# Mamba mixer on one core: the input norm moved to the end of the chunk two ahead of its own

## What is computed

```
def _ln_c(v, eps=1e-6):                      # over the 384 channels
    m = jnp.mean(v, axis=1, keepdims=True)
    s = jnp.var(v, axis=1, keepdims=True)
    return (v - m) / jnp.sqrt(s + eps)

xz = xseq @ in_proj_w.T                      # xseq = _ln_c(x); 384 -> 2 x 768
xin, z = jnp.split(xz, 2, axis=-1)
u = silu(causal_conv3(xin) + conv_b)         # per channel, 3 taps
dbc = u @ x_proj_w.T                         # dt (24), B (16), C (16)
dt = softplus(dt @ dt_proj_w.T + dt_proj_b)
# per position, 768 channels x 16 states:
h = exp(dt * A) * h + (dt * u) * B
y = sum_n h * C
out = x + ((y + u * D) * silu(z)) @ out_proj_w.T
```

## Time and profile before

| what | value |
|---|---|
| median of 3 runs | 3678.46 us (3677.39 to 3678.49) |
| profiled execution: span, first to last instruction | 3674.1 us |
| busy in the span: PE, DVE, ACT, POOL | 3352.4, 3256.0, 2759.3, 2577.3 us |
| the same, share | 91%, 89%, 75%, 70% |
| mean granted TensorE clock | 0.969 of 2.4 GHz |

### The profile page before, as it was taken

One profiled execution on the slowest core, in us unless ns is written; L12 is line 12 of the kernel. 1 busy time (PEld: TensorE's weight loads), 2 busy tenths in 40 slices (PEclk: granted clock), 3 DMA queues, 4 the chain that ended last, 5 costly groups with the idle time before them and its releaser, 6 DMA issues. The chain is left out here.

```text
span 3674.1 us, 50128 instructions
## 1 busy us (share of the span) xinstructions
PE 3352.4 (91%) x16962; PEld 2370.5 (65%) x16962; DVE 3256.0 (89%) x3376; ACT 2759.3 (75%) x5350; POOL 2577.3 (70%) x2045
## 2 busy tenths in 40 slices
PE   6989989899999989899989989898889998889997
PEld 3666666666666666666666666666657776557776
DVE  3999999999999999999999999999967887876886
ACT  5888797888789788977978787888655554875553
POOL 3898988989898988989898988989921111551100
PEclk7999999999999999999999999999999999999998
DMA  3020211202020211202020210202111113641212
GB/s 134 10 92 19 92 38 65 85 18 85 19 92 19 92 47 55 84 18 85 19 98 23 83 69 33 84 19 85 63 58 35 53 53 143 236 184 40 70 36 87
DMA packets 83586, 249.89 MB, mean 68 GB/s; under 512 B 15212, under 2 KB 24044, under 8 KB 73092
## 3 DMA queue, kind: packets, MB, share of 16 engines
q1 hardware_dynamic: 82564, 245.65, 18.6%
q10 hardware_dynamic: 768, 1.05, 0.1%
HBM read 204.73 MB, written 41.95 MB: 67 GB/s over the span
## 5 line engine op out<-in xcount | busy, mean ns | idle before, releaser
L956 POOL TENSOR_TENSOR slot<-dtu,b_rep 128x512 f32<-128x512 f32 x960 | 1206.4, 1277 | 78.5 <-PE ysum L454 77.8
L966 POOL TENSOR_TENSOR slot<-slot,c_rep 128x512 f32<-128x512 f32 x768 | 974.1, 1278 | 157.3 <-ACT carry L763 92.5
L454 PE MATMUL ysum<-ident,slot 128*128 128x128 f32 x6144 | 831.4, 280 | 31.9 <-POOL slot L966 16.7
L454 PEld LDWEIGHTS ysum<-ident,slot 128*128 128x128 f32 x6144 | 725.9, 145 | 173.0 <-issue 103.1
L754 ACT ACTIVATE state<-dt,aneg 128x512 f32<-128x512 f32 x960 | 655.4, 688 | 237.9 <-DVE slot L1065 200.8
L1065 DVE TENSOR_TENSOR slot<-state,c_rep 128x512 f32<-128x512 f32 x768 | 514.3, 672 | 0.0
L572 PEld LDWEIGHTS state<-diag_b,dtu_t 128*128 128x128 f32 x3072 | 385.0, 194 | 130.3 <-issue 121.1
L572 PE MATMUL state<-diag_b,dtu_t 128*128 128x128 f32 x3072 | 422.7, 281 | 33.0 <-ACT carry L763 16.6
L745 ACT ACTIVATE slot<-dt,aneg 128x512 f32<-128x512 f32 x576 | 405.4, 711 | 23.1 <-PE ysum L454 23.0
L1057 DVE TENSOR_TENSOR_SCAN slot<-state,slot 128x512 f32<-128x512 f32 x288 | 343.3, 1209 | 44.1 <-ACT state L754 33.6
L1057 DVE TENSOR_TENSOR_SCAN slot<-state,carry,slot 128x512 f32<-128x512 f32 x288 | 360.6, 1269 | 6.3 <-POOL slot L956 3.3
(11 more groups left out here) (272 smaller groups left out, 6291.9 us busy)
## 6 DMA issues: line engine op xcount, KB each, us to landing
c_rep<-rows_of_b_and_c SPq DMA_DIRECT2D x64, 1024.0 KB, 5.1
xres_l<-between_layers SPq DMA_DIRECT2D x18, 1536.0 KB, 9.8
xn_l<-between_layers SPq DMA_DIRECT2D x13, 1536.0 KB, 7.1
b_rep<-rows_of_b_and_c SPq DMA_DIRECT2D x16, 1024.0 KB, 4.5
between_layers<-y SPq DMA_DIRECT2D x10, 1536.0 KB, 6.4
xn<-in_x SPq DMA_DIRECT2D x16, 768.0 KB, 4.5
b_rep<-rows_of_b_and_c SPq DMA_DIRECT2D x16, 768.0 KB, 4.1
xres<-in_x SPq DMA_DIRECT2D x16, 768.0 KB, 4.5
```

Source lines behind the costliest of these rows:

```text
L454: last = mm(ysum[:, cols], slot[:, (NS * k + n) % SLOTS, cols], ident[:], start=first and j == 0, stop=final, is_transpose=True, skip_grou ...
L956: tt(slot[:, q % SLOTS], dtu[:, k % 2], b_rep[:, b_row(n)], ALU.mult).then_inc(dbu_done, 1)
L966: tt(slot[:, q % SLOTS], slot[:, q % SLOTS], c_rep[:, n], ALU.mult).then_inc(pool_mult_done, 1)
```

## The change

The norm of chunk d = c + 2 now stands at the end of chunk c, at steps 81 (mean), 86 (center), 90 (square), 89 (variance), 95 (rstd) and 93 (scale), for c = 0 to 13. Only the norm of chunk 1 stays where it was, in chunk 0 (`FIRST_NORM_AT`). The squares go into `acc`, the convolution's three tiles, which are free once the silus of chunk c + 1 are through; so the residual's load no longer waits for the variance, only for the store before it. The turn of B moves from step 80 to 83, the first turn of dt u from 84 to 87. Waits for py are exchanged: the mean waits for the fifth gate's silu, the output projection into py for the norm, the first in-projection for a residual copy. All instructions are the same in number and size.

```diff
--- before.py
+++ after.py
@@ -36,7 +36,8 @@
 OUT_IN, RES_AT = (BX, BY, BX), (13, 14, 22)
 LAST_OUT_IN, EARLY_OUT_AT, LATE_OUT_AT = (BX, BY, BZ), (88, 82, 84), (89, 90, 91)
 X_SUM_AT = 86
-MEAN_AT, CENTER_AT, SQUARE_AT, VAR_AT, RSTD_AT, SCALE_AT = 18, 21, 25, 25, 31, 28
+MEAN_AT, CENTER_AT, SQUARE_AT, VAR_AT, RSTD_AT, SCALE_AT = 81, 86, 90, 89, 95, 93
+FIRST_NORM_AT = (18, 21, 25, 25, 31, 28)
 GATE_AT, GATE_IN = (20, 22, 37, 49, 62, 70), (BX, BZ, BY, BX, BY, BZ)
 IN_AT, IN_IN = (28, 33, 34, 39, 45, 47), (BY, BZ, BX, BX, BY, BZ)
 CONV_IN_AT, CONV_AT = (33, 38, 41, 46, 50, 54), (31, 37, 40, 45, 50, 51)
@@ -48,8 +49,8 @@
 DT_ADD_AT = (67, 72, 77, 92, 30, 38)
 EARLY = 4
 DT_U_AT = 4
-TURN_U_AT, COPY_U_AT = (84, 13, 29, 44, 60, 75), (95, 20, 36, 48, 68, 84)
-TURN_B_AT, COPY_B_AT = 80, 90
+TURN_U_AT, COPY_U_AT = (87, 13, 29, 44, 60, 75), (95, 20, 36, 48, 68, 84)
+TURN_B_AT, COPY_B_AT = 83, 90
 DIAG_AT = (91, 94, 4, 9, 2, 7)
 HALO_AT = 20
 
@@ -168,7 +169,7 @@
         halo_mid = sb("halo_mid", [P, KT, 1])
         halo_bias = sb("halo_bias", [P, KT, 2])
 
-        sq = xres
+        sq = acc
         xp = sb("xp", [P, T])
         rl = sb("rl", [P, EARLY, T])
         dt = sb("dt", [P, KT, T])
@@ -244,9 +245,7 @@
 
             def load_res(b, h):
                 c = 2 * b + h
-                if not isinstance(c, int) or c < NCHUNK - 1:
-                    sp.wait_ge(var_full, c + 2)
-                else:
+                if later(c):
                     sp.wait_ge(x_stored, 16 * c)
                 nc.sync.sem_inc(res_free, 1)
                 sp.dma_start(xres[:], XV[b, :, :, h * T:(h + 1) * T]).then_inc(xres_loaded, 16)
@@ -327,7 +326,7 @@
             def norm_mean(d, h, image):
                 pe.wait_ge(x_loaded[h], 16 * (image + 1))
                 if later(d, 1):
-                    pe.wait_ge(res_done, CT * (d - 2) + 2)
+                    pe.wait_ge(z_read, KT * (d - 2) + 5)
                 if isinstance(d, int) and d == 1:
                     pe.wait_ge(dt_read, 2)
                 for t in range(CT):
@@ -343,6 +342,8 @@
             def in_proj(d, h, m):
                 if m == 0:
                     pe.wait_ge(normed, d + 1)
+                    if later(d, 1):
+                        pe.wait_ge(res_done, CT * (d - 2) + 2)
                 if m == 1 and later(d):
                     pe.wait_ge(u_copied, KT * (d - 1) + 3)
                 if m == 2 and later(d):
@@ -429,7 +430,10 @@
                         pe.wait_ge(out_w_in, 16)
                         pe.wait_ge(gated, KT * c + KT - 1)
                     if k == 0 and m == 1:
-                        pe.wait_ge(z_read, KT * (c + 1))
+                        if c < NCHUNK - 2:
+                            pe.wait_ge(normed, c + 3)
+                        else:
+                            pe.wait_ge(z_read, KT * (c + 1))
                     if k == 0 and m == 2 and banks == OUT_IN:
                         pe.wait_ge(res_done, CT * c + 1)
                     if k == 0 and m == 2 and banks != OUT_IN:
@@ -609,10 +613,14 @@
                             gate_proj(c, h, k)
                         if after and q == IN_AT[k]:
                             in_proj(d, 1 - h, k)
-                    if after and q == MEAN_AT:
-                        norm_mean(d, 1 - h, b + h)
-                    if after and q == VAR_AT:
-                        norm_var(d)
+                    if c == 0 and q == FIRST_NORM_AT[0]:
+                        norm_mean(1, 1, 0)
+                    if c < NCHUNK - 2 and q == MEAN_AT:
+                        norm_mean(c + 2, h, b + 1)
+                    if c == 0 and q == FIRST_NORM_AT[3]:
+                        norm_var(1)
+                    if c < NCHUNK - 2 and q == VAR_AT:
+                        norm_var(c + 2)
                     if after and q == XP_AT:
                         x_proj(d, 1 - h)
                     if not after:
@@ -665,8 +673,8 @@
 
             def norm_square(d, h):
                 act.wait_ge(centered, d + 1)
-                if later(d, 1):
-                    act.wait_ge(x_stored, 16 * (d - 1))
+                if later(d):
+                    act.wait_ge(u_done, KT * d)
                 af(sq[:], xn[:, h], ACT.Square).then_inc(squared, 1)
 
             def norm_rstd(d):
@@ -859,10 +867,14 @@
                                     set_diag(c, h, i)
                             elif after:
                                 set_diag(d, 1 - h, i)
-                    if after and q == SQUARE_AT:
-                        norm_square(d, 1 - h)
-                    if after and q == RSTD_AT:
-                        norm_rstd(d)
+                    if c == 0 and q == FIRST_NORM_AT[2]:
+                        norm_square(1, 1)
+                    if c < NCHUNK - 2 and q == SQUARE_AT:
+                        norm_square(c + 2, h)
+                    if c == 0 and q == FIRST_NORM_AT[4]:
+                        norm_rstd(1)
+                    if c < NCHUNK - 2 and q == RSTD_AT:
+                        norm_rstd(c + 2)
                     for k in range(KT):
                         if q == DT_READ_AT[k] and (after or k >= EARLY):
                             dt_read_tile(d if k < EARLY else c, k)
@@ -1100,10 +1112,14 @@
                         recur(b, h, (q + 1) // NS, (q + 1) % NS)
                     if q % NS not in POOL_N:
                         times_c(c, q // NS, q % NS)
-                    if after and q == CENTER_AT:
-                        norm_center(d, 1 - h, b + h)
-                    if after and q == SCALE_AT:
-                        norm_scale(d, 1 - h)
+                    if c == 0 and q == FIRST_NORM_AT[1]:
+                        norm_center(1, 1, 0)
+                    if c < NCHUNK - 2 and q == CENTER_AT:
+                        norm_center(c + 2, h, b + 1)
+                    if c == 0 and q == FIRST_NORM_AT[5]:
+                        norm_scale(1, 1)
+                    if c < NCHUNK - 2 and q == SCALE_AT:
+                        norm_scale(c + 2, h)
                     for k in range(KT):
                         if after and q == CONV_AT[k]:
                             conv(d, k)
```

## The result

| | kernel before | kernel after |
|---|---|---|
| median | 3678.47 us (4 runs) | 3709.02 us (4 runs, 3704.49 to 3709.91) |
| ratio to before, 95% interval | | 1.0083 [1.0069, 1.0097] |
| span of the profiled execution | 3674.1 us | 3707.4 us |
| mean granted clock | 0.969 | 0.968 |

The account below looks back on a forecast made before the run. PE was taken as full early in a chunk, DVE late. Costs 11.3 less gains 7.5 a chunk pair gave 27 us over seven pairs, plus 10 for the clock: 3715 us, range 3658 to 3735 (8 in 10).

Parts of the forecast that it names:

- gain, h = 0: Front of chunks where PE waits for ACT's carry copies: norm's work and waits leave DVE, less ACT's late decays; 3.3 us.
- gain, h = 1: Front of chunks where drives wait for no carries: norm's work and waits leave DVE; 4.2 us a chunk.
- cost at the end, h = 0: End of chunks whose PE waits for carry copies: two DVE passes, 3.34, plus three waits, less POOL's; 6.9 us.
- wait of step 87 there: Chunk end: DVE's scan of 87 waits for PE's drive behind the mean; 1.3 us (h = 0), 0.9 (h = 1).
- wait of step 94 there: Chunk end, h = 0: DVE's scan of 94 waits for PE's drive behind square, carries, variance and sums; 1.15 us.
- wait of the scaling there: Chunk end: DVE's scaling waits for ACT's Exp, Ln standing behind the dtu copy; 1.7 us (h = 0), 0.2 (h = 1).
- POOL's waits gone: Chunk end, h = 0: DVE's old waits for POOL, 0.47 and about 0.1, vanish under the new ones; -0.6 us.
- cost at the end, h = 1: End of chunks whose drives wait for no carries: two DVE passes, 3.34, plus waits of 0.9 and 0.2; 4.4 us.
- clock at the heads: Next chunk's head: PE's output projection may run at half clock after idling; 0.7 us a chunk, bounds 0 and 1.6.
- Interleaving pays: Rival: DVE's front waits go, chunk end absorbs the six links, if new waits stay under 2.0 us; 3651 us, chance 0.22.
- Work only moves: Rival: DVE is fullest, its work stays the same and new waits equal old; 3678 within 7 us, chance 0.13.
- Late PE grows: Rival: half clock after PE's idle at h = 0 chunk ends (11 us) and at every head (13 more); 3740 us, chance 0.15.

Follow-up runs that it names:

- e1: The kernel after the change, with the mean at step 84 instead of 81, behind PE's drive for step 87; 3734.99 us, 1.0158 of the kernel before.
- e3: The kernel after the change, with the rstd (Ln and Exp) at step 94 instead of 95, ahead of the dtu copy; 3688.38 us, 1.0034 of before.
- e6: The kernel after the change, with the square at step 91 instead of 90, behind the carry copies; 3720.31 us, 1.0112 of the kernel before.
- e7: The kernel after the change, with square at 91, variance at 88 and scaling at 95; 3675.97 us, 0.9994 of the kernel before.
- e12: The kernel after the change, with mean 83, center 87, square 91, variance 89, rstd and scaling at steps 1 and 3 of the next chunk; 3645.32 us, 0.9911 of before.

## Why the prediction was right

The forecast was 3715 us, +37; measured are 3709.0, +30.5 by the medians and +33.3 by the profiled spans. Term by term, us a chunk:

| term | predicted | measured |
|---|---|---|
| gain, h = 0 | 3.3 | 3.45 |
| gain, h = 1 | 4.2 | 4.46 |
| cost at the end, h = 0 | 6.9 | 7.0 |
| wait of step 87 there | 1.3 | 1.35 (1.20 to 1.47) |
| wait of step 94 there | 1.15 | 1.59 (1.03 to 1.75) |
| wait of the scaling there | 1.7 | 1.33 |
| POOL's waits gone | -0.6 | -0.53 |
| cost at the end, h = 1 | 4.4 | 4.3 |
| wait of step 87 there | 0.9 | 0.77 (0.71 to 1.07) |
| wait of the scaling there | 0.2 | 0.10 |
| clock at the heads | 0.7 | 9.0 / 14 = 0.64 |

*The gains.* The waits for PE went and ACT gave back what was said: 0.76 + 0.79 at steps 24 and 25 for a predicted 1.5, 0.37 at step 32 within the predicted 0.3 to 0.6. The tenths that the prediction gave to semaphores were too many: with h = 0, 5.68 us of waits and work less 2.11 of new waits (0.19 of them before the convolution's product of step 32) is 3.57, for 3.48 measured in chunk 8. The rule of the Trainium skill ("Perfetto Trace Analysis", section on identifying the most-contended engine) judges TensorE by its weight loads, which puts DVE first here; as the prediction works it out, only DVE's own 3.34 us would have come forward. The trace gives 0.11 more with h = 0 and 1.12 more with h = 1, 8.6 us over fourteen chunks, so the rule did not decide here, though with h = 0, where ACT took the waits back, it comes close.

*The costs.* Each of the three named waits stood where it was named. e1 shows the mean as the cause of the first and e3 the copy of dtu ahead of Ln as that of the third. The cause of the second is not shown apart. The prediction has it as a chain: square ahead of the carry copies, then drives, variance and two sums ahead of the drive of 94. The trace of the change shows that order; moving the square alone (e6) did not remove the wait, and e7, which removed it with h = 0, moves square, variance and scaling at once. No run moves the variance alone, and e12, with the variance at 89 as in the change but mean and square later and center 87, still waits 0.62 us there.

*Where the working was off.* First, the wait of 0.9 at step 87 with h = 1 was laid to the order of mean and drive alone. The row it was computed from, the drive at 1366.10, already held a half-clock stretch: the clock in that stretch of the kernel before is 0.87. e3 shows the same order to cost 0.0 at full clock and 0.72 behind half clock. So this wait, 5.4 us in all, needs the clock beside the order, and the number was right by luck: the kernel before had that stretch at half clock in three of the seven chunks, the change in all seven. With it the clock has a part in some 14 of the 33 us, and not in a quarter of them. The waits with h = 0 hold some of it too: that of step 94 is 1.03 us in chunk 0, which is at full clock behind the 3.58 us of idle PE, and 1.51 to 1.75 in the other six, which are not.

Second, the clock at the heads is no 0.7 a chunk: it is 0 in ten chunks and 1.7 to 2.8 in four, all above the upper bound of 1.6. That their sum comes near 14 x 0.7 is luck. e1 and e6 have it in 13 chunks and e12 in none, so the bounds for the whole (0 and 1.6 x 14 = 22 us) were the honest statement; e1 measured 20.3 and e6 22.2.

Third, one of its signs failed: a chunk was to last 165 to 168 us, and those with h = 0 last 167.6 to 170.9, those with h = 1 163.7 to 165.4. The other signs came as named, give or take two tenths: the wait of step 87 in all fourteen chunks, none before the centering but chunk 0's old one, and PE's first idle time at step 34.

*The rivals.* "Interleaving pays" failed for this table of steps and holds for another. What the prediction gave as its condition, new waits of DVE under 2.0 us a chunk, decides in fact: counted as the prediction counts, at the end and at the front, the change has 4.25 + 1.92 us in chunks 6 and 8 with h = 0 and 0.82 + 0.69 with h = 1 in chunk 7, 3.8 on the mean; e12 has 0.62 at the end with h = 0 and none with h = 1, and with the same waits at the front that is 1.6. That e12's 3645 us lies near the 3651 computed for this rival shows less, since e12 doesn't let the end of the chunk take in all six links: two stand at the next head, where the waits of steps 7 to 11 cover most or all of the pass. (The Trainium skill, "Perfetto Trace Analysis", section on optimization strategy, says that regimes with different most-contended engines may gain by being interleaved; e12 agrees and the change shows that it isn't enough.) "Work only moves" needed the waits to be wrong by their size. "Late PE grows" held in small: the matmuls behind the 3.58 us idle did run slow (1.09 us for four records of L573 at 1227.74, 0.60 at 1231.14), but they were short, the variance behind them ran in 2.74 us at full clock, and the wait of 94 is 0.5 to 0.7 us above that of chunk 0, not 1.6.

## What to carry to other kernels

A chain moved into another engine's holes pays only if every link has slack in the queue that it lands in: look at what stands directly behind each moved piece (here a drive of 1.05 us behind a mean of 2.74, a carry copy of 0.19 behind a square of 1.48, Ln behind a copy that waits for the last drive) and who wants it when. Put short and urgent work ahead of long and patient work, and put a pass where its engine waits anyway, even if that is in the next iteration: with the same instructions the places alone made 3735, 3709 and 3645 us. And before a row is used as a duration or as the start of a sum, look at the granted clock it was taken at.
